# Three stages on one core: closer meetings, and a causal mask added in the maximum pass

## The reference

```
x = x + 0.5 * ffn(layernorm(x), Wr, br, W1, b1, W2, b2)
x = x + attention(layernorm(x), Wqkv, Wo)
x = x + 0.5 * ffn(layernorm(x), Wr, br, W1, b1, W2, b2)
```

## Time and profile before

| | |
|---|---|
| median of 3 runs | 2317.75 us (2311.3 to 2318.44) |
| profiled execution | 2319.83 us, span 2318.0 us |
| TensorE (PE) busy | 2144.1 us, 92%, 18194 instructions |
| VectorE (DVE) busy | 1918.2 us, 83%, 3973 |
| ScalarE (ACT) busy | 1357.1 us, 59% |
| GpSimd (POOL) busy | 1297.5 us, 56% |
| all maxima, L978 | 838.4 us busy, 1408 of them, 141.6 us idle before them |
| all mask products, L1135 | 343.5 us busy, 1408 of them |
| issue to landing, median | k or q stack 4.5 us, image 3.5 us, x of the attention 4.1 us |

### The profile page before, as it was taken

The page is one execution under the profiler, slowest core; times in us unless marked ns, Lnnn a source line. Parts: engine busy times, 40 slices in busy tenths (PEclk is TensorE's granted clock), DMA queues, the critical chain, the costliest instruction groups (busy, mean ns, idle before and its releaser), DMA issues. The chain is left out here.

```text
span 2318.0 us, 53405 instructions
## 1 busy us (share of the span) xinstructions
PE 2144.1 (92%) x18194; PEld 1161.3 (50%) x18194; DVE 1918.2 (83%) x3973; ACT 1357.1 (59%) x2568; POOL 1297.5 (56%) x1460
## 2 busy tenths in 40 slices
PE   5999999889999999999999999999999987999999
PEld 2666665434444444444444444444444434666666
DVE  6777778688999899899989988998999855777776
ACT  3545554266666666666766666666666554455553
POOL 6666667354555455455545544554555435666664
PEclk9999999799999999999999999999999998999999
DMA  6666665444445445444544444444445422566665
GB/s 205 205 200 197 200 213 174 109 85 88 96 96 100 93 93 97 88 92 96 101 92 96 93 96 92 93 97 88 98 95 101 103 74 89 180 204 203 204 205 165
DMA packets 280391, 295.32 MB, mean 127 GB/s; under 512 B 45784, under 2 KB 263224, under 8 KB 280120
## 3 DMA queue, kind: packets, MB, share of 16 engines
q1 hardware_dynamic: 280120, 291.90, 49.8%
HBM read 140.08 MB, written 83.89 MB: 97 GB/s over the span
## 5 line engine op out<-in xcount | busy, mean ns | idle before, releaser
L1045 ACT ACTIVATE probs<-bank 128x512 f32<-128x512 f32 x1280 | 748.3, 604 | 471.9 <-PE bank L1153 465.4
L978 DVE TENSOR_REDUCE at_mx<-bank 128x1 f32<-128x512 f32 (+3 forms) x1408 | 838.4, 633 | 141.6 <-PE bank L1135 141.6
L899 POOL TENSOR_SCALAR_AFFINE_SELECT probs<-probs 128x512 f32<-128x512 f32 x512 | 319.0, 635 | 681.4 <-ACT probs L1045 677.8
L1153 PE MATMUL bank<-stacks 49*128 49x512 f16 (+3 forms) x2048 | 459.9, 302 | 73.3 <-ACT probs L1045 70.9
L1130 PE MATMUL bank<-stacks 48*128 48x512 f16 (+3 forms) x2048 | 495.2, 304 | 24.2 <-DVE at_mx L978 16.7
L1153 PEld LDWEIGHTS bank<-stacks 49*128 49x128 f16 x2048 | 135.7, 94 | 462.0 <-ACT probs L1045 338.7
L1135 PE MATMUL bank<-mask,turn 64*128 64x128 bf16 (+2 forms) x1408 | 343.5, 244 | 0.0
L622 ACT ACTIVATE turned<-bank,b1s 128x512 f32<-128x512 f32 x128 | 88.1, 688 | 189.1 <-PE bank L698 187.2
L698 PE MATMUL bank<-stacks 128*128 128x512 f16 x768 | 177.7, 389 | 22.6 <-DVE stacks L562 20.6
L1130 PEld LDWEIGHTS bank<-stacks 48*128 48x128 f16 x2048 | 158.5, 94 | 73.1 <-DVE at_mx L978 46.9
L905 POOL TENSOR_TENSOR turned<-turned,at_sin 128x512 f32<-128x512 f32 x128 | 176.5, 1379 | 33.0 <-DVE turned L953 33.0
(11 more groups left out here) (135 smaller groups left out, 4294.1 us busy)
## 6 DMA issues: line engine op xcount, KB each, us to landing
stacks<-qk_image SPq DMA_DIRECT2D x384, 128.0 KB, 4.5
qk_image<-v_qk SPq DMA_DIRECT2D x128, 256.0 KB, 3.5
stacks<-w_hi SPq DMA_DIRECT2D x192, 128.0 KB, 3.6
stacks<-w_lo SPq DMA_DIRECT2D x192, 128.0 KB, 3.8
b2s<-in_b SPq DMA_DIRECT2D x128, 128.0 KB, 3.7
after_ffn<-probs SPq DMA_DIRECT2D x32, 512.0 KB, 6.5
at_x<-after_ffn SPq DMA_DIRECT2D x32, 512.0 KB, 4.1
late_x<-after_ffn SPq DMA_DIRECT2D x32, 512.0 KB, 4.6
```

The costliest lines, as they stand in the source:

```text
L899: nc.gpsimd.affine_select(out=ap, in_=ap, compare_op=ALU.is_ge, fill=0.0, base=0, pattern=[[0, d] for d in dims] + [[1, P]], channel_multi ...
L978: nc.vector.tensor_reduce(o_ap, i_ap, AX_X, ALU.max).then_inc(max_done, 1)
L1045: nc.scalar.activation(probs[:, c, :], st_ps[c % 2][:], ACT.Exp, scale=DH ** -0.5).then_inc(exp_done, 1)
L1153: ins = nc.tensor.matmul(bank[:, col:col + T - q0], k_stack[ss.par][rows, j + ha, kt * P:(kt + 1) * P], q_stack[ss.par][rows, j + ha, q0:T ...
```

## The change

1. *Mask.* For n 0 to 3 the mask product is left out. VectorE's pass becomes a tensor_tensor_reduce that adds a table `over` (0, and -1e30 above the diagonal in its last 128 columns), writes the sum back to the bank and delivers the maximum. n 4 to 10 keep the product. GpSimd makes the table in the last lead-in slot, in `xn[1]`'s memory.
2. *Tables.* The waits for cosine and sine move from `start` to the first rope.
3. *First meeting.* `f1.store(B - 2)` goes behind all lead-in slots.
4. *Second meeting.* x(3) of the second ffn (and every fourth after it) goes into the attention's x buffer; x(2) and x(3) are loaded in slot over 1. Three blocks of `times_w1(0)` go between the scores of slot over 0 and `transposes(1)` into slot over 1. `norm(1)` goes behind slot (end, 3) and waits for the last maximum, since it overwrites the table.
5. *Second routing.* It is taken apart and put into steps 1 to 6 of the second ffn.

```
     def maxima(s, g, n):
             if n < 4:
-                o_ap, i_ap = out[:, n, 3:4], bank[:]
-            elif n < 8:
+                i = 3 - n // 4
+                w = (i + 1) * P
+                nc.vector.tensor_tensor_reduce(out=bank[:, 0:w], in0=bank[:, 0:w], in1=over[:, T - w:T], scale=1.0, scalar=LOWEST,
+                                               op0=ALU.add, op1=ALU.max, accum_out=out[:, n % 4, i:i + 1]).then_inc(max_done, 1)
+                return
+            if n < 8:
...
     def max_scores(s, g, n):
+            if n < 4:
+                nc.tensor.matmul(bank[:, 0:w], q_stack[s.par][rows, j + n % 4, i * P:(i + 1) * P],
+                                 k_stack[s.par][rows, j + n % 4, 0:w], start=True, stop=True).then_inc(mx_done, 1)
+                return
...
     gpsimd slot
+            if G == -1:
+                pool.wait_ge(first.xT_done, NC * B)
+                nc.gpsimd.memset(over, 0.0).then_inc(over_zeroed, 1)
+                pool.wait_ge(over_zeroed, 1)
+                nc.gpsimd.affine_select(out=over[:, T - P:T], in_=over[:, T - P:T], compare_op=ALU.is_ge, fill=-1e30,
+                                        base=0, pattern=[[-1, P]], channel_multiplier=1).then_inc(over_done, 1)
...
     begin_rope (VectorE), rope (GpSimd)
+            if idx == 0:
+                dve.wait_ge(tables_loaded, 32)
...
     sync, first meeting
                 if s == FIRST_LEAD - 1:
                     at.start()
-                if s == B - 1:
-                    f1.store(B - 2)
                 lead_in(at, s)
+            f1.store(B - 2)
             f1.store(B - 1)
...
     sync, second meeting
             at.slot(over, 1)
+            f2.load_x(2)
+            f2.load_x(3)
             f2.second_ahead()
             at.slot(over, 2)
-            f2.load_x(2)
             at.slot(over, 3)
             at.slot(over + 1, 0)
-            f2.load_x(3)
             at.finish()
...
-                if s == SECOND_ROUTING:
+                if s == SECOND_ROUTING + 5:
                     f2.routes(1)
...
     gpsimd
             at.slot(end, 2)
+            at.slot(end, 3)
             f2.norm(1)
-            at.slot(end, 3)
...
     vector, in the steps of the second ffn
                 if s == SECOND_ROUTING:
-                    f2.route(1)
+                    f2.route_rows(1)
+                if s == SECOND_ROUTING + 2:
+                    f2.route_turned(1)
+                if s == SECOND_ROUTING + 3:
+                    f2.route_top(1)
...
     tensor
+            def w1_between(n):
+                if n in (3, 5, 7):
+                    f2.times_w1(0, [(n - 3) // 2])
+            def turns_between(n):
+                if n == 4:
+                    f2.transposes(1)
...
-            at.slot(over, 0)
-            f2.times_w1(0, range(3))
-            at.slot(over, 1)
+            at.slot(over, 0, w1_between)
+            at.slot(over, 1, turns_between)
             f2.times_w1(0, range(3, 4))
-            f2.transposes(1)
             at.slot(over, 2)
...
             f2.times_w2(0)
-            f2.route(1)
             for s in range(2, B):
                 f2.step(s)
+                if s == SECOND_ROUTING + 2:
+                    f2.route_turn(1)
+                if s == SECOND_ROUTING + 3:
+                    f2.route_logits(1)
```

More of the change, by code:

```diff
@@ L30 @@
 HALF = 0.5
+LOWEST = -3.0e38
 HP = P // 2
@@ L142, in __init__ @@
         self.row, self.row_n = sb("row", [B, D], F32), sb("row_n", [B, D], F32)
+        self.at_x = sb("at_x", [P, NT, D], F32)
         self.ones = sb("ones", [H // 2, T], F16)
@@ L166, in of_last_ffn @@
         rows = lambda pair: pair.rearrange("p a (b d) -> p (a b) d", d=D)
[L167 removed]
+        x = [self.x[0], self.x[1], self.late_x[0], self.at_x]
         xT = [self.xT0, Split(s0[:, 4:6, :], s0[:, 6:8, :])]
@@ L352, in load_x @@
                 sp.wait_ge(before.stored[s % 2], 16 * (s // 2 + 1))
-                if s in (2, 3):
-                    sp.wait_ge(before.stored[s % 2], 16 * (B // 2))
+                if s == 2:
+                    sp.wait_ge(before.stored[0], 16 * (B // 2))
+                if s == 3:
+                    sp.wait_ge(before.xn_done, NT * B)
             sp.dma_start(x[s % NX][:].rearrange("p t d -> p (t d)"), src_v[s]).then_inc(x_loaded[s % NX], 16)
@@ L482, in norm @@
             pool.wait_ge(rstd_done, s + 1)
+            if before and s == 1:
+                pool.wait_ge(before.max_done, 44 * B)
             pool.sem_inc(norm_starts, 1)
@@ L652, in route_logits @@
             pe.wait_ge(r_Tcopied, 2 * k + 1)
+            if k:
+                pe.wait_ge(xT_lo, NC * (route_at(k) + 1))
             pe.wait_ge(wr_loaded, 32)
@@ L665, in transposes @@
             wait(pe, xT_lo, NC * s)
-            for k in range(len(batches)):
+            if s == 0:
+                pe.wait_ge(r_Tcopied, 2)
+            for k in range(1, len(batches)):
                 if s == route_at(k):
+                    pe.wait_ge(r_Tcopied, 2 * k + 1)
+                if s == route_at(k) + 1:
                     pe.wait_ge(r_Tcopied, 2 * k + 2)
@@ L733, in route_at @@
     def route_at(k):
-        return 0 if k == 0 else SECOND_ROUTING + 2
+        return 0 if k == 0 else SECOND_ROUTING + 4
     own = Phase(sync=sync, gpsimd=gpsimd, vector=vector, scalar=scalar, tensor=tensor)
-    own.stored, own.xT_lo, own.gelu_done, own.out_done = stored, xT_lo, gelu_done, out_done
+    own.stored, own.xT_lo, own.gelu_done, own.out_done, own.xT_done = stored, xT_lo, gelu_done, out_done, xT_done
     return own
@@ L748, in attention @@
     q_stack, k_stack, v, qk, (swapped, by_cos, by_sin, rotated), ones = mem.of_attention()
-    x = sb("x", [P, NT, D], F32)
+    x = mem.at_x
     xn = sb("xn", [P, NT, D], F32)
@@ L758, in attention @@
     probs, on, res = mem.probs, mem.on, mem.late_x
+    over = mem.xn[1][:].rearrange("p t d -> p (t d)")[:, 0:T]
     o32 = sb("o32", [P, T], F32)
@@ L780, in attention @@
     rows_set = [sem(f"rows_set{i}") for i in range(2)]
+    over_zeroed, over_done = sem("over_zeroed"), sem("over_done")
     src_v = src.rearrange("b (t p) d -> b p t d", p=P)
@@ L904, in rope @@
             pool.wait_ge(rope_in, idx + 1)
+            if idx == 0:
+                pool.wait_ge(tables_loaded, 32)
             nc.gpsimd.tensor_tensor(by_sin[t % 2][:], swapped[t % 2][:], sin_t[:], ALU.mult).then_inc(sin_done, 1)
@@ L963, in maxima @@
             dve.wait_ge(mx_done, 11 * G + n + 1)
+            if G == 0 and n == 0:
+                dve.wait_ge(over_done, 1)
             if n == 0:
@@ L1252, in project_o, with slot @@
                 ins.then_inc(o_done, 1)
-        def slot(s, g):
+        def slot(s, g, between=None):
             G = 4 * s.b + g
@@ L1265, in slot @@
             for n in range(11):
+                if between:
+                    between(n)
                 if run and n < 10:
@@ L1299, in attention @@
     own.st_done, own.pv_done, own.qk_lo, own.k_written = st_done, pv_done, qk_lo, k_written
-    own.max_done, own.on_done = max_done, on_done
+    own.max_done, own.on_done, own.xn_done = max_done, on_done, xn_done
     own.res_done, own.exp_done, own.mt_copied = res_done, exp_done, mt_copied
@@ L1419, in _ @@
                 f2.step(s)
-                if s == SECOND_ROUTING:
+                if s == SECOND_ROUTING + 1:
                     f2.route(1)
```

2 lines of the change are left out of this document (removed).

## The result

The changed kernel takes 2289.72 us (median of 4 runs, 2287.27 to 2299.74), the kernel before 2318.1 (4 runs, 2311.3 to 2327.29). The ratio is 0.9874, 95% interval 0.9846 to 0.9902: faster by 1.3%. The forecast of 2308 had the sign, and the time lies inside its range (2284 to 2346), but it was 18 us too high, and the time is that of rival B. The profiled execution took 2291.23 us (span 2289.5), 28.5 us less of span than before. Where the 28.5 us are is read first.

The account below looks back on a forecast made before the run. VectorE was taken to pace about half of an attention sample, TensorE g=3, the start of g=0 and the feed-forwards. -12.3 + 20.4 - 3 - 7.5 - 8 = -10.4 us gave 2309.4 profiled, 2308 timed; range 2284 to 2346.

Parts of the forecast that it names:

- rival B: Attention's maximum pass: the fused pass costs no more than the reduction, only the gains stand; 2288 (2280 to 2298), chance 0.24.
- Products gone, -12.3: Attention, slots g=3 and g=0: mask products leaving TensorE save 0.41 us a sample over 30 samples, -12.3 us.
- New pass, +20.4: Attention's maxima on VectorE: 8.5 fused passes a sample cost 0.08 us more each, over 30 samples +20.4 us.
- Tables of the rope, -3: First feed-forward: the wait for cosine and sine moves to the first rope, saving 3 us (0 to 5).
- First meeting, -7.5: First feed-forward to attention: earlier k reads start slot 0 4.5 us sooner, full clock there saves 3; -7.5 (-3 to -11).
- Second meeting, -8: Attention to second feed-forward: moved blocks, transposes, x(3) load and routing together save 8 us (-3 to -12).
- (a): Attention to second feed-forward: three w1(0) blocks go between the scores of slot over 0, saving 2 us.
- (b): Attention to second feed-forward: transposes(1), 1.9 us, goes into slot over 1, saving 1.5 us.
- (c): Second routing: TensorE's 9.37 us stand ahead of w1(2) and VectorE's 6.54 us for x(3) go; late weights remain.
- C: Attention's maximum pass: fetching the maximum or writing the bank costs 0.15 to 0.25 us a pass; 2325 to 2362, chance 0.26.
- D: Mask costs as in the forecast, but the meetings give back what they gain; about 2320 us, chance 0.12.
- A: The forecast itself: 0.08 us more per fused pass, meetings as worked out; 2298 to 2318 us, chance 0.38.

Follow-up runs that it names:

- store_back: The changed kernel with f1.store(30) ahead of the last lead-in slot again: 2296.85 us, ratio 0.9871 to the kernel before.
- tables_back: The changed kernel with the waits for cosine and sine at start again: 2295.30 us, ratio 0.9902 to the kernel before.
- filler: The changed kernel with ten unused TensorE products of 512 columns between the first ffn's last w2 block and attention slot 0: 2290.32 us, ratio 0.9854.
- hybrid: The changed kernel with the mask product and plain reduction again in the slots g=2 alone: 2288.43 us, ratio 0.9838 to the kernel before.

## Why the forecast was half right

- *Products gone, -12.3.* Right in kind, a little small: 0.44 us a sample with the fused pass and 0.52 with the plain reduction, instead of 0.41. With the plain reduction the absent products bring 0.13 us in g=1 too, though VectorE looked full there (10.43 of 10.53 us in the earlier trace rows).
- *New pass, +20.4.* This term failed: 8.5 passes at 0.08 us. The place was right (the passes of g=1 and g=2, 8 of them), the price was 0.021 us, so +5.1 us for 30 samples. That is under the break-even of 0.05 us of the forecast, so the mask gains 10.5 us in 30 samples instead of costing 8. I had looked for the price of a second instruction in a pair whose second part starts 0.08 us after the first, and charged that distance. In the trace the read starts when the pass would have let the next operation start anyway, and the next operation starts with it. The end of the range that I called B (+0) was nearer. With 5.1 in place of 20.4 and 0.52 in place of 0.41 the sum is 2319.8 - 15.6 + 5.1 - 18.5 = 2290.8, near the profiled time (2291.2); the closeness is in part luck, since the -18.5 were -22.7 by the edits' own rows and +4.3 elsewhere.
- *Table of the mask, 0.* VectorE's first pass, at 427.70, waits for the scores (PE bank L1158) and not for the table.
- *Tables of the rope, -3.* Measured 2.7 to 4.3 in two profiles against the mean of twelve.
- *First meeting, -7.5.* The size is about right (7.9 by store_back against the mean, 5.4 in the one profile of the changed kernel). The split isn't: the start moved by some 2.8 us and not 4.5. I let k's image land 3.5 us after its issue, a median over the whole kernel, where these two DMAs took 5.7 to 5.9 us before the change already; tables_back, where the tables give nothing, shows the reads at 419.89 and slot 0 at 428.39, not 418 and 427. That slot 0 starts at 427.29 in the changed kernel, near my 427, is luck: there the first ffn also ends 1.6 us earlier, which is counted under the tables. The sentence "without the gap slot 0 runs at full clock" failed twice: the gap stayed at 2.26 us, and without it (filler) the clock falls some 5 us later all the same. Why the ten kernels with the store moved reach G=4 sooner than the two without stays open beyond the 2.8 us.
- *Second meeting, -8.* Measured 10.9 to w1(2): (a) and (b) 3.2 (3.5 forecast), (c) 6.5 by x(3)'s load (by exclusion; 4.5 forecast), and 1.2 that go with the clock and that no run here settles. For (b) I had read 1.9 us off transposes that ran at half clock; at full clock they take 1.06 us, so the near hit of the sum of (a) and (b) is luck in part. The remaining gap is 3.7 us, of late weights as said: w1(2) starts 5.1 us after their issue, and I had allowed 6.9.
- *The rivals.* B, at 0.24, is what happened (2288). C fell with the price of the pass. D fell: the meetings gave 18.4 us and more, not 5. What decided between A and B was one price, and no row of the kernel before had it; the 0.38 and 0.24 were a fair picture of that, but the value should have been taken between the ends.

## What to carry to other kernels

A second instruction in the trace costs what it shifts the start of the next one, not its length: price it start to start. When an engine is relieved and another one pays, put the gain and the price each in the slots where that engine sets the pace; here both came in the slots named (and the gain in one more), though the price per pass was a quarter of the forecast. A DMA's landing time is to be read at the place in question and not from a median of the whole kernel: 5.8 us stood against 3.5 here. When a long stand before an instruction goes away with several edits, undo them one by one: the named releaser (the routing's row) was itself waiting for a DMA, and moving it was worth at most 0.5 us of some 7.

## What the runs showed of the hardware beyond that

A kernel's scatter goes with the granted clock. Nine runs of the kernel before on one chip go from 2316.5 us at a mean clock of 0.986 to 2333.6 us at 0.975. From 500 to 1800 us every profile has the clock at 1.00; near the second meeting, 1820 to 1880 us, it differs from kernel to kernel though their work is nearly the same. Windows of that stretch in the changed kernel, and then in hybrid:

```profile
1820.00:1880.00 60.00, 48.42 (x418) 21.23 (x416) 44.92 (x118) 31.05 (x63) 19.06 (x31) 0.91 0.22 49
```

```profile
1820.00:1880.00 60.00, 51.52 (x366) 21.10 (x363) 39.98 (x104) 27.50 (x54) 17.03 (x28) 0.72 0.13 41
```

From G=120 to G=127 it takes 84.5 us in the first and 91.6 in the second. It is 91.3 us in store_back too, whose code there is the changed kernel's, so the difference isn't hybrid's edit. So an edit worth 3 us can't be read from four totals here; it can from a mark at full clock. A fused pass that starts right behind another takes 0.65 us at 512 elements and 0.52 at 384 to the next start. Behind another operation it is 0.61 and 0.47, and where a fused pass of 512 had to wait before it started, 0.62, behind another fused pass too. Why isn't settled.
